# First layer of a four-part network: another order of one round on TensorE, VectorE and ScalarE

## The reference

```python
def softmax_kernel(x, proj, is_query):
    norm = x.shape[-1] ** (-0.25)
    ratio = proj.shape[0] ** (-0.5)
    xp = jnp.einsum('bhnd,md->bhnm', x * norm, proj)
    diag = jnp.sum(jnp.square(x), axis=-1, keepdims=True) * 0.5 * (norm * norm)
    if is_query:
        stab = jnp.max(xp, axis=-1, keepdims=True)
    else:
        stab = jnp.max(xp, axis=(-1, -2), keepdims=True)
    return ratio * (jnp.exp(xp - diag - stab) + EPS_K)
...
q, k, v = split(video @ Wq.T + bq), split(video @ Wk.T + bk), split(video @ Wv.T + bv)
qp, kp = softmax_kernel(q, proj, True), softmax_kernel(k, proj, False)
denom = jnp.einsum('bhnm,bhm->bhn', qp, jnp.sum(kp, axis=2))
ctx = jnp.einsum('bhnm,bhnd->bhmd', kp, v)
out = jnp.einsum('bhnm,bhmd->bhnd', qp, ctx) / denom[..., None]
attn = out.transpose(0, 2, 1, 3).reshape(b, n, d) @ Wo.T + bo
x = layer_norm(video + attn, g2, be2)
ff = jax.nn.relu(x @ W1.T + b1) @ W2.T + b2
return layer_norm(x + ff, g3, be3)
```

## Time and profile before

| | |
|---|---|
| median of 3 runs | 1882.97 us (1881.5 to 1886.79) |
| the profiled execution | 1877.83 us, span 1876.1 us |
| first layer within the span | 0 to 364 us |
| TensorE, VectorE, ScalarE, GpSimd busy over the span | 82%, 68%, 55%, 42% |

### The profile page before, as it was taken

The page is one execution under the profiler, slowest core; times in us unless marked ns, Lnnn a source line. Parts: engine busy times, 40 slices in busy tenths (PEclk is TensorE's granted clock), DMA queues, the critical chain, the costliest instruction groups (busy, mean ns, idle before and its releaser), DMA issues. The chain is left out here.

```text
span 1876.1 us, 26759 instructions
## 1 busy us (share of the span) xinstructions
PE 1531.1 (82%) x8752; PEld 970.7 (52%) x8757; DVE 1278.9 (68%) x3228; ACT 1024.1 (55%) x1747; POOL 786.3 (42%) x902
## 2 busy tenths in 40 slices
PE   4788787279999999677459999999998585999990
PEld 2444554247666666443125555555553574777770
DVE  2557656367777777466758877778883483788875
ACT  2345544315666665534425767677766553677762
POOL 2133333344555554324751112221100377488875
PEclk8899898658999999978867999999999598999995
DMA  7600000132222221000053544444430011444425
GB/s 215 229 1 1 1 1 1 38 98 71 71 71 71 71 72 42 3 12 1 1 127 99 129 126 117 119 104 113 120 89 2 24 61 55 139 136 120 134 59 135
DMA packets 96202, 144.30 MB, mean 77 GB/s; under 512 B 31267, under 2 KB 59940, under 8 KB 91953
## 3 DMA queue, kind: packets, MB, share of 16 engines
q1 hardware_dynamic: 91072, 134.11, 25.8%
q0 software_dynamic: 4992, 8.48, 1.4%
HBM read 104.19 MB, written 57.48 MB: 86 GB/s over the span
## 5 line engine op out<-in xcount | busy, mean ns | idle before, releaser
L1193 DVE TENSOR_REDUCE ctx_nm<-ctx_s 128x1 f32<-128x512 f32 x512 | 329.4, 681 | 95.5 <-PE ctx_s L1469 94.6
L1305 ACT ACTIVATE ctx_probs<-ctx_st 128x1024 f32<-128x1024 f32 x256 | 254.0, 1022 | 113.4 <-PE ctx_st L1485 109.0
L1193 DVE TENSOR_REDUCE rope_nm<-rope_s 128x1 f32<-128x128 f32 (+3 forms) x512 | 230.2, 481 | 86.1 <-PE rope_s L1472 84.0
L1305 ACT ACTIVATE rope_probs<-rope_st 128x1024 f32<-128x1024 f32 (+1 forms) x256 | 172.2, 702 | 138.5 <-PE rope_st L1485 137.3
L1469 PE MATMUL ctx_s<-ctx_kst,ctx_qst 96*128 96x512 f32 x512 | 220.0, 467 | 17.3 <-DMA ctx_kst<-ctx_contexts 8.4
L1469 PE MATMUL rope_s<-rope_kst,rope_qst 96*128 96x128 f32 (+3 forms) x512 | 185.2, 395 | 4.0 <-DVE rope_nm L1193 3.2
L1058 POOL TENSOR_SCALAR_AFFINE_SELECT rope_probs<-rope_probs 128x256 f32<-128x256 f32 x256 | 98.3, 409 | 170.0 <-ACT rope_probs L1305 169.5
L1469 PEld LDWEIGHTS ctx_s<-ctx_kst,ctx_qst 96*128 96x128 f32 x512 | 100.0, 196 | 131.2 <-DVE ctx_nm L1193 54.9
L1485 PE MATMUL ctx_st<-ctx_qst,ctx_kst 98*128 98x512 f32 x512 | 164.5, 404 | 2.4 <-ACT ctx_probs L1305 2.4
L1485 PE MATMUL rope_st<-rope_qst,rope_kst 98*128 98x512 f32 (+3 forms) x512 | 141.0, 359 | 3.9 <-ACT rope_probs L1305 3.9
L2665 DVE TENSOR_TENSOR sw_hl<-sw_hf,sw_hh 128x512 fp32r<-128x512 f32 x124 | 129.9, 1047 | 0.1
(11 more groups left out here) (382 smaller groups left out, 3354.3 us busy)
## 6 DMA issues: line engine op xcount, KB each, us to landing
sw_raw<-in_L_ffn_all SPq DMA_DIRECT2D x24, 768.0 KB, 4.5
sw_xs<-in_pad SPq DMA_DIRECT2D x65, 260.0 KB, 9.8
rope_halves<-rope_qk SPq DMA_DIRECT2D x24, 512.0 KB, 4.7
ctx_halves<-ctx_qk SPq DMA_DIRECT2D x24, 512.0 KB, 6.2
ctx_qst<-ctx_contexts SPq DMA_DIRECT2D x32, 384.0 KB
ctx_kst<-ctx_contexts SPq DMA_DIRECT2D x32, 384.0 KB
rope_qst<-rope_halves SPq DMA_DIRECT2D x32, 192.0 KB
rope_kst<-rope_halves SPq DMA_DIRECT2D x32, 192.0 KB
```

The costliest lines, as they stand in the source:

```text
L1193: nc.vector.tensor_reduce(nm[:, g, j * T + t:j * T + t + 1], bank("s", b, n)[:, 0:keys], AXX, ALU.max, negate=True).then_inc(s_used, 1)
L1305: nc.scalar.activation(probs[n // GH % 2][:, n % GH, u * units[0]:u * units[0] + units[u]], st_bank[u][:, 0:units[u]], ACT.Exp, scale=SCAL ...
```

## The change

Only the order of calls in three loops is changed; no instruction, buffer or semaphore is added or taken away.

- TensorE: turn_x1 and turn_input go to the front of the round, ahead of the first two key products; project q goes ahead of the last two key products; contexts go ahead of turn_lengths; attend goes ahead of narrow.
- VectorE: divide goes ahead of with_x1; residual goes from behind divide to behind with_input.
- ScalarE: keep_lengths goes between the two query exponents; keep_contexts goes ahead of the first norm (normalise 1).

```diff
@@ TensorE
             for b in rounds:
                 m, f, a, e = b, b + 1, b - 1, b - 2
-                if within(m):
-                    key_features(m, 0)
-                    key_features(m, 1)
                 if within(e):
                     turn_x1(e)
                 if within(f):
                     turn_input(f)
                 if within(m):
+                    key_features(m, 0)
+                    key_features(m, 1)
+                if within(f):
+                    project(f, "q")
+                if within(m):
                     key_features(m, 2)
                     key_features(m, 3)
                 if within(a):
                     output(a)
-                if within(f):
-                    project(f, "q")
                 if within(m):
                     turn_maxima(m)
...
                 if within(f):
                     lengths(f)
+                if within(m):
+                    contexts(m)
+                if within(f):
                     turn_lengths(f)
                 if within(m):
-                    contexts(m)
                     turn_queries(m)
                     turn_contexts(m)
+                if within(m):
+                    attend(m)
                 if within(e):
                     narrow(e)
-                if within(m):
-                    attend(m)
@@ VectorE
+                if within(a):
+                    divide(a)
                 if within(g):
                     with_x1(g)
-                if within(a):
-                    divide(a)
-                if within(b - 4):
-                    residual(b - 4)
                 if within(m):
                     largest_keys(m)
...
                 if within(a):
                     with_input(a)
+                if within(b - 4):
+                    residual(b - 4)
                 if within(m):
                     shift_keys(m)
@@ ScalarE
                 if within(m):
                     query_exponents(m, 0)
+                if within(f):
+                    keep_lengths(f)
+                if within(m):
                     query_exponents(m, 1)
                 if within(f):
-                    keep_lengths(f)
                     place_lengths(f)
                 if within(f2):
                     input_norm(f2)
                 if within(m):
                     keep_queries(m)
+                if within(m):
+                    keep_contexts(m)
                 if within(a):
                     normalise(1, a, x1, r, n1_ready)
-                if within(m):
-                    keep_contexts(m)
```

## The result

The changed kernel takes 1867.38 us (median of 4, 1865.08 to 1869.23) beside 1882.59 us of the kernel before: a ratio of 0.9915 with a 95% interval of 0.9897 to 0.9933. That is 15.2 us less; 8.3 were forecast. The range (1861 to 1884) holds it and the sign is right, the size is short by nearly half.

What follows compares the result with a forecast made beforehand. No engine is full; a chain through several sets the period, with TensorE's largest wait for dgT. Terms -20.4 - 1.5 - 0.5 - 7.4 + 4.8 + 16.2 + 0.5 = -8.3 us gave 1874.7 us, range 1861 to 1884.

Steps and rivals of the forecast that it cites:

- What bounds the kernel; lengths and contexts: Rounds 0 to 6: the wait for dgT and half-rate contexts go, query copies behind the input norm bound next; -20.4 us.
- Attend ahead of narrow: Full rounds: the oT wait is covered but the next thing is as late, 0 in rounds 3 to 6; round 1 gains -1.5.
- End of the layer: From round 7's front to the layer's end: earlier spread product, query products, attend and statistics ahead of the residual; -7.4 us.
- Where turning ahead costs: TensorE waits for y in round 0 (+3.6) and for x1 in round 2 (1.2 reaches L276); +4.8 us.
- The clock: Rounds 0 to 5: a new stall before the third query transposes slows attend and part of narrow to half rate; +16.2 us.
- The residual: On VectorE, moved behind with_input, it meets GpSimd's inverse root and waits for it alone; +0.5 us for all rounds.
- rival B: The residual waits for GpSimd's inverse root and both squares: 4.3 us more, 1879 us; chance 0.18.
- Rival A: The clock holds through the new stall, so its 16.2 us aren't paid: 1858.5 us; chance 0.20.
- C: Rounds 2 to 5: the half rate outlasts narrow, 18 us over four rounds, slower than before: 1893 us; chance 0.10.

Runs made afterwards that it cites:

- v_queries: The changed kernel with ScalarE's input norm moved behind the first norm, so that the query copies follow place_lengths at once; ratio 0.9792 to the kernel before.
- v_attend: The kernel before with only attend ahead of narrow, keep_contexts ahead of the first norm and divide ahead of with_x1; ratio 0.9958.
- v_noturn: The changed kernel with turn_x1, turn_input and project q back in their old places; ratio 0.9913 to the kernel before.
- v_fill: The changed kernel with 28 unread products (16 in round 0) ahead of the third group of query transposes in rounds 0 to 5; ratio 0.9925.
- v_qmask: v_queries with mask_contexts also moved ahead of the statistics of x2 on VectorE; ratio 0.9771 to the kernel before.
- v_nores: The changed kernel with the residual back behind divide and with_x1 on VectorE; ratio 0.9931 to the kernel before.
- v_fill2: The changed kernel with 13 unread products (7 in round 0) filling the stall before the third group of query transposes; ratio 0.9817 to the kernel before.
- v_after: The changed kernel itself, profiled a second time; ratio 0.9907 to the kernel before.

## Why the prediction was right or wrong

**What bounds the kernel; lengths and contexts: right.** The term was -20.4. Left columns of the table, m = 0 to 6: -20.7. Round 6 alone, forecast 6.3, gave 6.28. That the next bound is the copy behind the input norm, 3.1 us on and not 6, is shown by the 3.65 us wait and by v_queries.

**Attend ahead of narrow: right, in full rounds.** The term was 0, and v_attend gives 0.1 of 37.6. Whether the turns stand ahead decides what is left of the wait for r2: 0.19 with them, 0.88 without (v_noturn). Round 7's front came to 2.13, forecast 2.1.

**End of the layer: right in kind, sizes off both ways.** Round 7's spread product in the kernel before, on which the term rests, and which no row ahead of it shows:

```profile
293.52 0.39 PE L276 MATMUL pf_dve<-pf_diag,pf_unit 16*128 16x16 f32 x2 [1.97 <-DVE pf_r L587]
```

Query products of round 7 at the full clock (before, it was 0.50 over 294 to 297): 1.4 where 0.4 was taken. Behind the last copy: 3.5 where 4.9 was taken, since two stalls there now brought half rate on both last narrow stages, which take 5.47 us where they took 3.84 before. In v_fill and v_qmask both take 3.84 behind the same stalls, and the way from the copy to the end is 51.9 in place of 53.5: with the clock up the gain is 5.1. Where the 4.9 came from was taken wrongly: attend ahead of narrow was to give 2.9 and gives 0.2 without the residual's move (v_attend), the residual was to give 2.0, and without its move 3.6 is lost (v_nores). TensorE in the last rounds:

```profile
312.11 5.47 PE L383 MATMUL pf_held<-pf_w,pf_hT 128*128 128x128 f32 x32 [2.87 <-ACT pf_hT L737]
...
325.74 5.47 PE L383 MATMUL pf_held<-pf_w,pf_hT 128*128 128x128 f32 x32 [1.90 <-ACT pf_hT L737]
```

The same two in v_fill:

```profile
322.04 3.84 PE L387 MATMUL pf_held<-pf_w,pf_hT 128*128 128x128 f32 x32 [2.87 <-ACT pf_hT L741]
...
335.68 3.84 PE L387 MATMUL pf_held<-pf_w,pf_hT 128*128 128x128 f32 x32 [1.90 <-ACT pf_hT L741]
```

**Where turning ahead costs: mis-sized.** Round 0 was to lose 3.6 and lost 1.9. TensorE in round 0:

```profile
35.72 1.09 PE L248 MATMUL pf_act<-ident,pf_y 128*128 128x128 f32 x4 [2.10 <-ACT pf_y L662]
...
40.79 1.88 PE L264 MATMUL pf_held<-pf_feats,pf_kT 128*128 128x512 f32 x4
...
44.87 0.39 PE L276 MATMUL pf_dve<-pf_diag,pf_unit 16*128 16x16 f32 x2
```

The wait for y is there (2.10), and the last key products come 2.8 later than before (the 0.6 of the later load taken off), as worked out. But L276 follows them after 4.1, not 5.0: project q was counted where it went to and not where it was taken from. Round 2's new wait of turn_x1 was forecast to last until 4.3 after attend's start, and does (94.54 to 98.85). TensorE from the end of round 1 into round 2:

```profile
94.54 3.55 PE L348 MATMUL pf_held<-pf_qpT,pf_cx 128*32 128x512 f32 x16 [0.47 <-ACT pf_cx L724]
...
98.85 0.63 PE L248 MATMUL pf_act<-ident,pf_x 128*128 128x128 f32 x4 [0.76 <-POOL pf_x L459]
...
106.94 0.39 PE L276 MATMUL pf_dve<-pf_diag,pf_unit 16*128 16x16 f32 x2 [0.27 <-DVE pf_r L589]
```

From attend to L276 it is 12.4, what the forecast has without any loss of clock. v_noturn shows what the term left out: the turns ahead of the key products cover with_x1 in every round. By the layers compared there they are worth 3 to 6 us in the sum, where I had put them at a loss of 4.8.

**The clock: the step that failed most.** The mechanism is shown (v_fill2 against the changed kernel), the term of +16.2 was too large. In rounds 2 to 5 it is 1.4, 2.4, 2.4 and 2.9, 9.1 in all, where 11.2 stood; in round 0 1.55 where 1.5 stood. In round 1, 3.5 was taken and 0.8 came (16.18 from copy to L276, against 15.41 in v_queries, where attend runs at its full rate): attend did slow down to 3.55, but turn_x1 waited for GpSimd in any case, and the clock was back (from 98 on) when the key products came. Time lost under a wait that ends later costs nothing, and I had added the two. That makes 11.4 of the 16.2. In the changed kernel's second profile (v_after) the half rate in round 4 was short, and the way from copy to L276 18.8 in place of 20.2 with the same order: the price belongs to an execution, not to a kernel.

**The residual: no cost.** The term was +0.5; rival B had it wait for three operations. In v_nores, where the residual stands in its old place, full rounds take the same as in v_after. VectorE's r and residual, then GpSimd's inverse root and first square, in round 4:

```profile
178.12 0.69 DVE L589 TENSOR_TENSOR pf_r<-pf_dve,pf_yb 128x512 f32<-128x512 f32 x1
...
178.85 0.69 DVE L603 TENSOR_TENSOR X<-X,pf_x 128x512 f32<-128x512 f32 x1
...
178.26 1.02 POOL L438 TENSOR_TENSOR pf_rstd<-pf_mv,pf_half 128x4 f32<-128x4 f32 x1 [9.12 <-DVE pf_mv L515]
...
179.25 1.19 POOL L445 TENSOR_TENSOR pf_sqq<-pf_qT 128x512 f32<-128x512 f32 x1
```

The residual took 0.69, its usual time, though it started 0.43 before the inverse root ended. It was the square that grew, 1.19 in place of the 1.04 that it takes in round 3, which has no residual; rounds 5 and 6 show the same 1.19. By the Trainium skill, SBUF — State Buffer, section "Who interferes with whom", the inverse root, which reads SBUF, would have held off a VectorE instruction with two SBUF inputs to its end; this trace speaks against that for an operation of 4 elements a partition, as far as a GpSimd span of the profile can be trusted to 0.4 us. With the affine part in round 9 (512 elements, residual 1.37) it agrees; the square grew by 0.15, about half of the 0.29 in which it ran beside the residual.

**In sum.** Too much taken: clock 2.1 and 2.7, round 0 1.7, residual 0.5; too little: round 7's query products 1.0; the other way, the end of the layer 1.4 and the later load 0.6. With 8.3 that makes 14.3 of the 15.0; 0.3 more lies in the left columns and 0.4 in rounds 2 to 5, whose way from copy to L276 is 17.82 with the clock up (v_fill2) where it was 17.93. Rival A (the clock holds, 1858.5) fell by the 0.61 above. C (the half rate outlasts narrow) fell since the clock was back at 1.00 from 204 on, while round 4's narrow still ran (202.49 to 206.88), and full rounds took 37.4 at most. B fell by the residual. The time came out between the forecast and A mostly because the clock was costed as if all of it lay on the path: 4.8 of the 6.7 missed.

## What to carry to other kernels

When a wait is taken away, look in the row of the engine that answers next: the idle time ahead of its instruction is about the gain (2.96 here, and the copy moved by 3.05), and the instruction queued ahead of it is the next thing to move; here one more such move was worth more than the whole change. A step that moves must be entered twice in the sum, where it goes and where it leaves. And a slowed stretch costs only what isn't under a wait that ends later anyway.

## What the runs showed of the hardware

A VectorE residual with two SBUF inputs ran at its usual 0.69 us beside GpSimd's inverse root over 4 elements a partition, which it overlapped by 0.43, but took 1.37 beside an operation over 512 (v_nores). The granted clock fell at other places in two profiles of the same kernel (at 0.50 behind round 4's stall for about four us in v_after, for some seven in the changed kernel's first profile), and once in a full round whose longest wait was 1.0 us (v_fill2, near 176), so that sums over the layer repeat only within 2 to 3 us, while single stretches away from it repeat to 0.1. A product of 32-bit operands shows as two instructions in the trace (56 for 28 in v_fill).
